# An expert loop of 71 steps written out, and token counts moved ahead of twelve weight matmul pairs

## What is computed

```python
logits = xf @ gate_w.T                       # 4096 tokens, 8 experts
weights, indices = top_k(logits, 2); weights = softmax(weights)
for e in range(8):
    h = silu(xf @ w1[e].T) * (xf @ w3[e].T)  # 128 -> 384
    out += combine[:, e:e + 1] * (h @ w2[e].T)
```

## Time and profile before

| | us |
|---|---|
| median of 3 runs | 527.25 (526.24 to 527.28) |
| the profiled execution, its own time | 526.45 |
| its span in the trace | 524.7 |
| TensorE busy | 390.1 (74%) |
| VectorE, GpSimd, ScalarE busy | 255.3, 246.8, 168.1 |
| mean granted TensorE clock | 0.877 |

### The profile page before, as it was taken

How to read it: one execution, slowest core, us unless ns; L and a number is a source line. 1 busy time by engine, 2 the same in 40 slices (tenths; PEclk the granted TensorE clock), 3 DMA queues, 4 the chain that set the end, 5 groups by cost and what they waited for, 6 DMA issues and landing times.

```text
span 524.7 us, 7887 instructions
## 1 busy us (share of the span) xinstructions
PE 390.1 (74%) x2272; PEld 319.2 (61%) x2273; DVE 255.3 (49%) x637; ACT 168.1 (32%) x387; POOL 246.8 (47%) x265
## 2 busy tenths in 40 slices
PE   0899899860999888699497877967878687886700
PEld 0565555650587767556397776867877587875700
DVE  5377664440789999729732322332323332333236
ACT  0544444020123231343043333333323333333233
POOL 7224423412774465100255655556556566664434
PEclk9999999795799999969587979797979988899855
DMA  8910000003001000730011111111111111111184
GB/s 247 223 40 2 0 0 0 6 5 35 2 0 41 20 20 21 280 141 1 15 36 41 47 33 43 35 39 41 35 40 40 40 35 45 40 44 31 36 303 178
DMA packets 14081, 29.94 MB, mean 57 GB/s; under 512 B 4392, under 2 KB 5564, under 8 KB 13548
## 3 DMA queue, kind: packets, MB, share of 16 engines
q1 hardware_dynamic: 7388, 17.93, 11.3%
q0 software_dynamic: 4784, 9.52, 6.7%
q10 hardware_dynamic: 1888, 2.23, 1.2%
HBM read 20.24 MB, written 8.85 MB: 55 GB/s over the span
## 4 chain that ended last, share of the span: by engine, by line
PE 50%; DVE 17%; issue 10%; DMA 6%; another core or an unknown queue 5%; ACT 5%; POOL 4%; SPq 1%; POOLq 1%; DVEq 0%; ACTq 0%
PE bank L953 14%; PE bank L935 11%; DVE xn L990 7%; PE bank L928 6%; PE bank L895 2%; DMA RS<-r_hl 2%; PE bank L783 2%; PE bank L922 2%; PE bank L726 2%; PE bank L734 2%; POOL shared L499 2%; ACT shared L676 2%; DVE st L980 1%; PE bank L914 1%
## 5 line engine op out<-in xcount | busy, mean ns | idle before, releaser
L524 POOL DMA_INDIRECT y_dram<-shared,idx_scatter x71 | 69.9, 985 | 80.0 <-DVE shared L1248 68.2
L935 PE MATMUL bank<-spec,shared 128*128 x426 | 71.6, 311 | 39.0 <-ACT shared L676 36.7
L519 POOL DMA_INDIRECT shared<-tn_dram,idx_gather x71 | 68.8, 969 | 58.8 <-DVE idx_gather L1238 37.4
L935 PEld LDWEIGHTS bank<-spec,shared 128*128 128x128 f32 x426 | 61.3, 216 | 46.1 <-issue 45.7
L1258 DVE TENSOR_TENSOR shared<-shared,bank 128x384 f32<-128x384 f32 x71 | 39.2, 552 | 70.6 <-issue 36.6
L1243 DVE TENSOR_TENSOR xgt_hl<-bank,xgt_hl 128x128 fp32r<-128x128 f32 x71 | 20.7, 291 | 90.2 <-ACT xgt_hl L671 85.1
L953 PE MATMUL bank<-RS,xgt_hl 128*128 x142 | 59.4, 419 | 0.1
L683 ACT ACTIVATE shared<-bank 128x384 f32<-128x384 f32 x71 | 34.8, 491 | 68.3 <-PE bank L953 49.1
L990 DVE TENSOR_SCALAR xn<-T,mv,rstd 128x128 f32<-128x128 f32 (+1 forms) x64 | 51.3, 872 | 3.7 <-POOL rstd L438 3.1
L953 PE MATMUL bank<-w_hi,xgt_hl 128*128 x142 | 51.8, 365 | 0.0
L671 ACT ACTIVATE xgt_hl<-bank 128x128 fp32r<-128x128 f32 x71 | 19.7, 277 | 75.7 <-PE bank L922 57.3
(11 more groups left out here) (175 smaller groups left out, 685.2 us busy)
## 6 DMA issues: line engine op xcount, KB each, us to landing
star<-y_dram SPq DMA_DIRECT2D x16, 256.0 KB, 5.5
star<-in_w SPq DMA_DIRECT2D x2, 1536.0 KB, 8.4
tn_dram<-xn SPq DMA_DIRECT2D x8, 256.0 KB, 2.0
out<-T ACTq DMA_DIRECT2D x8, 256.0 KB, 2.5
spec<-in_w SPq DMA_DIRECT2D x1, 1536.0 KB, 7.1
shared<-in_sp_even SPq DMA_DIRECT2D x1, 1280.0 KB, 14.6
shared<-tn_dram,idx_gather POOLq DMA_INDIRECT x71
y_dram<-shared,idx_scatter POOLq DMA_INDIRECT x71
```

The source lines that it names most:

```text
L519: pool.indirect_dma_start(xg[j % BUFS], None, tn_dram, bass.IndirectOffsetOnAxis(ap=idx_gather[:, j:j + 1], axis=0)).then_inc(S[f"g_x{j % ...
L524: pool.indirect_dma_start(y_dram, bass.IndirectOffsetOnAxis(ap=idx_scatter[:, j:j + 1], axis=0), yo[j % BUFS], None).then_inc(S[f"y_out{j ...
L935: mm = pe.matmul(p_y[:, 0:DIM], hidt[u][:, c * P:(c + 1) * P], w2s[:, c, ds(e * DIM, DIM)], start=(c == 0), stop=(c == HC - 1))
```

## The change

`tile_loop` becomes `tile_steps`, which writes all 71 steps out on PE, ACT and DVE; every wait then has a constant. In PE's routing part the two count matmuls and their waits stand ahead of all twelve chunks of low weights, where they stood between the fourth and the fifth. POOL's and SP's programs do not change.

```diff
-def tile_loop(eng, step):
-
-    for b in range(BUFS):
-        step(b, b)
-    with eng.Fori(1, SLOT_TILES // BUFS - 1) as n:
-        for b in range(BUFS):
-            step(n * BUFS + b, b)
-    for b in range(RUN_TILES - (SLOT_TILES - BUFS)):
-        step(SLOT_TILES - BUFS + b, b)
+def tile_steps(step):
+
+    for j in range(RUN_TILES):
+        step(j, j % BUFS)
...
-            tile_loop(act, lambda j, b: step(j, b % 2))
+            tile_steps(lambda j, b: step(j, b % 2))
...
             pe.wait_ge(S["w_neg"], 1)
             pe.wait_ge(S["b_logit"], PAIRS)
-            for k in range(4):
-                weight_rest(k)
             pe.wait_ge(S["q_tri"], 3)
             pe.wait_ge(S["q_ready"], 2)
             counts = q_cnt.bitcast(F16)[:, 0:TILES * E].rearrange("p (t e) -> p e t", e=E)
             pe.matmul(ps_tot[:, 0:E * TILES], ones[:, :], counts, start=True, stop=True).then_inc(S["q_count"], 1)
             pe.matmul(ps_rank[:, 0:E * TILES], tri[:, :], counts, start=True, stop=True).then_inc(S["q_count"], 1)
-            for k in range(4, len(w_chunks)):
+            for k in range(len(w_chunks)):
                 weight_rest(k)
...
-            tile_loop(pe, step)
+            tile_steps(step)
...
-            tile_loop(dve, step)
+            tile_steps(step)
```

## The result

| | before | after |
|---|---|---|
| median of 20 runs each, us | 527.26 | 529.46 |
| lowest and highest, us | 522.20 to 529.93 | 526.00 to 531.79 |
| ratio, 95% interval | | 1.0044 [1.0023, 1.0065] |
| the profiled execution, its own time | 526.45 | 528.03 |
| its span | 524.7 | 526.3 |

The changed kernel is slower by 0.44%, or 2.2 us. The interval excludes no change, though its lower end, 0.23%, is hardly more than the 0.2% that a measurement of this kernel can tell.

A forecast was written before the change was run, and what follows sets the result against it. No engine is full; VectorE's tables and TensorE's chunks together bound line 914, and inter-engine stops the expert loop. +3.5 for chunks and -0.5 for the loop gave +3.0 on the 527.25 median: 530.2 us, range 522.0 to 535.5.

The forecast's parts named there:

- Counts ahead of the chunks: Routing: twelve chunks instead of eight behind the counts on TensorE delay line 914's successor, +3.5 us (+1.9 to +5.1).
- the mis-sized term, the clock: Routing: TensorE's clock stays at 0.50 for 3.2 us after work begins at 232.60, losing 1.6 us.
- rival C: Routing: chunks do not hold line 914 back, only VectorE's earlier scan counts (-1.4): 525.3 us; chance 0.05.
- Branches and register work: Expert loop: seven turns lose a compare-and-branch and the waits' register values, -0.5 us (0 to -2.2).
- the stops: Expert loop: idle times of some microseconds, put down to traffic between engines; same size expected after the change.
- A: Expert loop: all first 41 steps run at the quick 3.216 us, gain 7.3 us: 522.9; chance 0.27.
- B: Expert loop: the pace follows its slow part, 17 steps lose 0.177 us each, +3.0: 533.2; chance 0.12.
- D: Expert loop: each hardware-loop turn fetched code, so unrolling saves 1.4 us in seven turns, -9.8: 520.4; chance 0.04.
- E: TensorE's longer program stalls on eight to thirteen more instruction blocks, +11 to +18 us: about 541 to 548; chance 0.05.
- The gap: Routing, sign of being right: TensorE idle from about 228.5 to 232.6 us, ahead of the counts.
- the bare start of line 907: Routing, sign of being right: line 907 starts at 247.9 without waiting for VectorE, idle time below 0.1 us.
- the later gather: After routing, sign of being right: the first gather comes 3.5 us later than before.

The follow-up runs named there:

- e1: Only the counts moved ahead of all chunks, hardware loop kept, against the kernel before: 529.85 us, ratio 1.0052.
- e2: Only the 71 steps written out, chunks and counts in the old order, against the kernel before: 526.22 us, ratio 0.9970.
- e4: e1 plus eight unused identity matmuls ahead of the wait for the counts: 529.11 us, ratio 1.0037 to the kernel before.
- e12: e2 with GpSimd's indirect scatter replaced by plain SyncE transfers to fixed rows, first chip: 456.99 us against 524.84 for the kernel before.
- e3: e2 with two chunks ahead of the counts, seven behind them, three behind the index products: 523.05 us, ratio 0.9882 to the kernel before.
- e5: Same edit as e12 (scatter replaced by plain SyncE transfers, on e2), second chip: 450.07 us against 471.83 for the kernel before.
- e9: The changed kernel without edit, on the third chip: 477.11 us against 471.45 for the kernel before, ratio 1.0117.

## Why the prediction was right

The forecast was +3.0 us, 530.2, in a range of 522.0 to 535.5, with slower as the likeliest sign. Measured: 529.46, +2.2. The mechanism was the one that e1 shows. How close the total came is in part luck: in the two traces the routing stage lost more than forecast and the loop stage gained more (+4.3 for +3.5, -2.9 for -0.5), which partly cancels; by medians e1 gave +2.5 and e2 -1.1.

- **Counts ahead of the chunks, +3.5 forecast (1.9 to 5.1).** The profile shows +4.3 from the gate to line 907, and e1 alone +3.8. The mechanism is the one named. Line 907 came 0.88 us after the 247.94 forecast. Of these, 0.09 is the later start of the counts, and 0.2 a slip in the sum: it let the eight chunks end at 244.22, where line 914 started only at 244.44, so that the order's share was 2.1 and not 1.9, as e4 has it. The rest, 0.6, is the mis-sized term, the clock. I let it stay at 0.50 for 3.2 us, the length seen before, at a cost of 1.6. It stayed for 5.4 us and cost 2.2 in the changed kernel (16.13 - 13.95), and for 4.3 us and 1.7 in e1 (15.63 - 13.95). What the prediction did not say is that 244.44 holds a clock loss of its own in the first four chunks; at full clock on both sides the order costs an estimated 3.7 us (e12).
- **The head start of VectorE (rival C)** came, at 2.2 us the upper end of the 1.5 to 2.2 forecast, and ended in the idle time of 6.88 us. C fell.
- **Branches and register work, -0.5 (0 to -2.2).** e2 gives -1.1 by the medians. The profiles show -2.9 from T8 to T70 in the changed kernel and -2.1 in e2, but +0.9 in e3 with the same loop, so single profiles scatter by more than the effect. Whether the 1.1 us come from the register work or from how the stops fall stays open.
- **The steps' pace (A and B).** After, 3.28 us a step, between the 3.393 and 3.216 of the earlier trace rows and close to their mean. Neither happened. These two took up most of the width of the range. The prediction said that the stops belong to the traffic between engines and not to the hardware loop; they stayed with constant waits, in the size of before, and left with the scatter in e12.
- **Each turn fetched code (D)** would have given -9.8. The loop alone gave -1.1. The prediction read the rule of the Trainium skill (Runtime: NRT & Kernel Launch, section Instruction fetch mechanics) too widely: it speaks only of a taken branch whose target lies outside the present window. The same section of the Trainium skill gives blocks of 256 instructions and a window of two, and for TensorE a memory of 2048. In the trace of before a turn has 359 recorded TensorE instructions, and by those figures it can stay inside. So the missing fetches of the earlier trace rows do not speak against the rule, and D had no ground in it.
- **The longer program (E)** brought 8 more blocks (19 for 11), at the lower end of the 8 to 13 forecast, with no loss that e2 shows.
- **What the profile would show.** The gap, the counts behind it, the bare start of line 907, the later gather (4.38 us instead of 3.5) and the stops are all there. The scan came at 233.78, earlier than the 234.5 that I had named.

The sum by profiles: +0.06 + 4.32 + 0.01 + 0.10 - 2.94 + 0.08 = +1.6 us, and by the separate kernels +1.4, beside +2.2 measured.

## What to carry to other kernels

On an engine that works in order, asking for an item early is only half of the move: what stood ahead of it must go behind the whole chain that waits next, not just behind the item. Here four chunks moved behind the counts landed in front of the index products and cost 2.5 us by themselves (e1), while two left in the gap and three put behind those products gain 3.2 against the same written-out loop (e3 and e2), 4.3 against before. When a gap is opened ahead of TensorE, count the clock's return with it: here it took 1.7 to 2.2 us of the routing stage, although filling the gap (e4) took only 0.7 off the total, inside the noise. A stage read from one profile can carry the luck of its clock. And compare kernels on one chip only.

## What the runs showed of the hardware

**The same kernel takes 527 us on one chip and 471 on two others.** The difference lies in the stage that mixes GpSimd's indirect transfers with TensorE's steps: for the changed kernel 203.41 us for 62 steps on the first and 157.23 on the third, and 22.18 and 16.47 for the eight steps ahead of them. Without the scatters both kinds take 135.04 for the 62. What in the chips or around them differs is open.

**With GpSimd's scatters go stops of other engines.** On the first chip ScalarE waits some 2 us for matmuls that have long ended, and an estimated 46 us of the loop's 203 (203.41 - 157.23) go by in such stops; they are gone when plain transfers on SyncE's queue replace the scatters (e12). One stop is left there, during a run of twelve gathers, where a step takes TensorE 8.2 us beside 2.2 in e5. On the other chips GpSimd's own cost bounds the loop instead: 0.97 us for a gather, 0.99 for a scatter, and 0.30 between instructions.

**The clock's return differs from one restart to the next.** Each of these stretches begins at 0.50. Counted from the first matmul of the unbroken work, the clock is back after 3.2 us in the kernel before (228.81 to 232.00) and 1.7 in e2 (228.53 to 230.2), with the same instructions in the same order; after 2.7 in e3, which has only two chunks there, and 1.7 in e4 with the small matmuls; and after 5.4 in the changed kernel (232.69 to 238.05), 4.3 in e1 and 5.9 in e9, the last three behind 4.15 us of idle time. In e12 it was up before the gate's last matmuls. The length taken from one such row, 3.2 us, gave a price of 1.6 us where 2.2 were paid.

**Not every matmul takes longer at 0.50.** From the first count matmul to the first chunk 0.88 us go by at either level, while a chunk takes 2.11 us at 0.50 and 1.1 at 1.00.
